# A language-model tower on one core: attention projections of ScalarE in two units, VectorE's steps behind them one unit on, and the output addition ahead of the cell

## The chip, the core and the metric

The kernel runs on one core of a Trainium2 chip. A core has five engines, each with its own instruction queue that it works off strictly in the order in which the program wrote it: TensorE (PE: matrix products), VectorE (DVE: element-wise work and reductions), ScalarE (ACT: activation functions), GpSimd (POOL) and SyncE (SP, here only the issuer of DMA transfers). Queues meet only through semaphores: an instruction that waits for one holds back everything behind it on its engine. The metric is the device time of one execution in microseconds (us).

## The reference

One layer of a small language model over 16 sequences of 512 tokens and a width of 128. Three parts follow each other for each sequence: an embedding with a short Fourier transform, a local attention with 64 summary tokens and 8 heads, and an LSTM as a mixture of 8 experts of which each token takes 2. The LSTM's scan runs over the sequences, so its state passes from sequence to sequence.

```
h = tok(x, ...)                                   # (16, 512, 128)
h = h + attn(_layernorm(h), W_qkv, b_qkv, W_out, b_out)
h = h + ffn(_layernorm(h), router_w, ..., Wi, Wh, b, Wo, bo)

attn:  Q, K, V = split(x @ W_qkv + b_qkv); Q = Q * SCALING
       aw  = softmax(Qw . Kcat);  out_wtok = aw . Vcat            # 64 summary tokens
       w_wtok = softmax(Qf . out_wtok);  w_fea = softmax(Qf . Kseg)  # a window of 17 keys
       out_fea = w_wtok * out_wtok + w_fea . Vseg
ffn:   top_vals, top_idx = top_k(logits, 2);  rw = softmax(top_vals)
       step: gates = xt @ Wi + h @ Wh + b;  i_, f_, g_, o_ = split(gates)
             c = sigmoid(f_) * c + sigmoid(i_) * tanh(g_);  h = sigmoid(o_) * tanh(c)
             y = h @ Wo + bo
```

## The kernel before

**Steps and units.** The main part runs over the 16 sequences (`STEPS`). A step is cut into 32 units (`NG * E`): 8 experts of 4 gates each, expert `e = t // 4` and gate `g = t % 4`. In every unit TensorE computes one gate of one expert for both of a token's choices (1024 columns; `unit_gate`, lines 594, 597 and 599), and ScalarE takes its tanh (`gate_tanh`, line 762). TensorE may be at most two gates ahead of ScalarE, since there are two PSUM halves for gates. VectorE closes an expert over the four units that follow: in a unit with `g == 1` the masked input and the swap of hidden states of the next expert (lines 1108, 1116) and `input_part` (1141), with `g == 2` `chosen` (1162) and `cell` (1149, 1153), with `g == 3` the swap of the cell state (1123), in the next `g == 0` `hidden` (1131). `hidden` needs ScalarE's tanh of the cell (`cell_tanh`, line 769), issued in the unit with `g == 3`.

**Front.** Beside the LSTM of one sequence, the embedding and the attention of the next ones are woven in, in small pieces (`front`). A table per engine (`PE_AT`, `ACT_AT`, `DVE_AT`, `SP_AT`) says in which unit a piece is written into that engine's queue. A negative number belongs to the step before: -5 is unit 27, -4 is unit 28, -3 is unit 29 there. `run_front` puts the pieces in. What sets the order is this table and the order of the calls inside `step` of each engine; there is no scheduler behind it. On VectorE the front piece of a unit stands behind `masked_input`, the swaps and `chosen`, and ahead of `input_part` and `cell`. On ScalarE it stands behind the unit's `gate_tanh` and `cell_tanh`, on TensorE behind the unit's gate.

**The pieces around the change.** TensorE computes query, key and value in unit 27 (line 524). ScalarE moves them out of PSUM: query `qT` (698) and two scaled halves of it, `qz` (703), then key `kw`, `kf` (707, 708) and value `vw`, `vf` (710, 711), all in one go in unit 27; `split` (716, 718) makes the f16 upper parts of key and value a unit later. VectorE waits for `qT` and `kf` for the products `pw` (921, 922), then makes the lower parts of the query (`q_lo`, 926) in unit 28, of key and value (`kv_lo`, 931, 934) in unit 29, and so on through `v_win` (942), `w_max` (946, 948), `s_max` (971), `s_sub`, `w_sum`, `w_out` (961 to 967), up to `p_T`. ScalarE's exponential for the summary tokens (721) waits for `w_max`. `add_y` (1168) adds the LSTM's output of the sequence before to its residual; it waits for four transposes of TensorE (`y_back`, line 618).

**The first step.** Step 0 has a single state per token (512 columns) and no forget gate. Ahead of it the front of sequence 0 and part of that of sequence 1 run alone. In every step a mask for each expert comes by DMA into `masks` before `masked_input` can use it.

Of the kernel before, what the change touches and what calls it, by code (L numbers as in the profile page):

```python
# [5 lines left out]
def lm_tower_kernel(nc, x_ids, frame_ids, emb_table, proj_w, proj_b, w_qkv, b_qkv, w_out, b_out,  # L6
# [46 lines left out]
    Q_SCALE = 2.0 ** 4  # L53


    SP_AT = dict(ids=-16, qbd=-3, vz=1, rows=25, wrow=28)
    PE_AT = dict(emb=-10, xT=-6, qkv=-5, summary=-2, window=0, feature=6, values=12, proj=15, projT=16, x2T=19,
                 logits=21, maskT=25)
    ACT_AT = dict(h=-10, xT=-6, qkv=-5, split=-4, summary=0, window=3, pr_hi=7, feature=8, proj=15, x2T=19,
                  choice=21, maskT=25)  # L60
    DVE_AT = dict(onehot=-14, moments=-9, xn=-8, pw=-4, q_lo=-4, kv_lo=-3, v_win=-2, w_max=-1, s_max=1, s_sub=2, w_sum=3,
                  w_out=4, s_sum=5, s_norm=6, f_max=7, p_lo=8, p_T=9, f_sum=10, f_part=10, attn=13,
                  moments2=16, xn2=17, x_lo=20, choice1=21, choice2=21, weights=22)
    EARLY = 16
    MASKS_AT = 26
    YT_AT, YBACK_AT, YADD_AT = 5, 6, 7
    WT0 = 64
    XM_AT = 30
    ENC0 = 32
# [2 lines left out]
    with ctx:  # L72
# [26 lines left out]
        rows = sb("rows", [P, SEQ])  # L99
# [7 lines left out]
        xn = sb("xn", [P, TILES, D])  # L107
# [7 lines left out]
        ids = prod[0:VOCAB, :].bitcast(i32)  # L115
# [10 lines left out]
        attn = sb("attn", [P, SEQ])  # L126
# [537 lines left out]
        def _(act):  # L664
# [18 lines left out]
            def front(t, b):  # L683
                b1 = b + 1
                if t == ACT_AT["h"]:
                    act.wait_ge(S["emb"], b1)
                    if not is_zero(b):
                        act.wait_ge(S["h2"], b)
                    A(h_sb[:, :, :].rearrange("p t d -> p (t d)"), FA[:, 0, :], ACT.Copy).then_inc(S["hsb"], 1)
                if t == ACT_AT["xT"]:  # L690
                    act.wait_ge(S["xnTp"], b1)
                    A(xnT[:, :], FA[:, 0, :], ACT.Copy).then_inc(S["xnT"], 1)
                if t == ACT_AT["qkv"]:
                    act.wait_ge(s_prep, 3)
                    act.wait_ge(S["qp"], b1)
                    if not is_zero(b):
                        act.wait_ge(S["S"], b)
                    A(qT[:, :], FA[:, 0, :], ACT.Identity, bias=bqkv_sb[:, 0:1], scale=DH ** -0.5).then_inc(S["q"], 1)
                    act.wait_ge(S["q"], b1)
                    if not is_zero(b):  # L700
                        act.wait_ge(S["mwp"], b)
                    for c in range(2):
                        last = A(qz[:, :, c, :, HI], qT[:, NW:SEQ].rearrange("p (j q) -> p j q", q=QB), ACT.Copy,
                                 scale=parq[:, c:c + 1])
                    last.then_inc(S["qhi"], 1)
                    act.wait_ge(S["kp"], b1)
                    A(kw[:, :], FA[:, 1, 0:NW], ACT.Identity, bias=bqkv_sb[:, 1:2])
                    A(kf[:, PAD:PAD + TF], FA[:, 1, NW:SEQ], ACT.Identity, bias=bqkv_sb[:, 1:2]).then_inc(S["k"], 1)
                    act.wait_ge(S["vp"], b1)
                    A(vw[:, :], FB[:, 0:NW], ACT.Identity, bias=bqkv_sb[:, 2:3])  # L710
                    A(vf[:, PAD:PAD + TF], FB[:, NW:SEQ], ACT.Identity, bias=bqkv_sb[:, 2:3]).then_inc(S["v"], 1)
                if t == ACT_AT["split"]:
                    if not is_zero(b):
                        act.wait_ge(S["mout"], 16 * b)
                    act.wait_ge(S["k"], b1)
                    A(khl[:, HI, :], kf[:, :], ACT.Copy, scale=Q_SCALE).then_inc(S["khi"], 1)
                    act.wait_ge(S["v"], b1)
                    A(vp16[:, :, HI], vf[:, :], ACT.Copy, scale=Q_SCALE).then_inc(S["vhi"], 1)
                if t == ACT_AT["summary"]:
                    act.wait_ge(S["dw"], b1)  # L720
                    A(ew[:, :], prod[:, :], ACT.Exp).then_inc(S["ew"], 1)
                if t == ACT_AT["window"]:
                    act.wait_ge(S["dS"], b1)
                    A(pr[:, :], pr[:, :], ACT.Exp, scale=1.0 / (Q_SCALE * Q_SCALE)).then_inc(S["eS"], 1)
                if t == ACT_AT["pr_hi"]:
                    act.wait_ge(S["pn"], b1)
                    A(pr16[:, :, HI], vwin[:, :], ACT.Copy, scale=V_SCALE).then_inc(S["phi"], 1)
                if t == ACT_AT["feature"]:
                    act.wait_ge(S["df"], b1)
                    A(ew[:, 0:TF], prod[:, 0:TF], ACT.Exp).then_inc(S["ef"], 1)  # L730
                if t == ACT_AT["proj"]:
                    act.wait_ge(S["projT"], b1)
                    A(xnT[:, :], FA[:, 1, :], ACT.Identity, bias=bout_sb[:, 0:1]).then_inc(S["projS"], 1)
                if t == ACT_AT["x2T"]:
                    act.wait_ge(S["x2p"], b1)
                    A(x32[:, :], FB[:, :], ACT.Copy).then_inc(S["x32"], 1)
                    A(xs[:, par_of(b), HI, :], FB[:, :], ACT.Copy, scale=V_SCALE).then_inc(S["xhi"], 1)
                if t == ACT_AT["choice"]:
                    act.wait_ge(S["dd"], b1)
                    A(m4[:, 6, :], m4[:, 5, :], ACT.Exp).then_inc(S["ed"], 1)  # L740
                if t == ACT_AT["maskT"]:
                    act.wait_ge(S["mwp"], b1)
                    if not is_zero(b):
                        act.wait_ge(S["mout"], 16 * b)
                    A(mrow[:, :], FB[0:K * E, :], ACT.Copy).then_inc(S["mrow"], 1)
                    if not is_zero(b):
                        act.wait_ge(S["wout"], 16 * b)
                        act.wait_ge(S["ybo"], b)
                    A(wT, FB[WT0:WT0 + E, :], ACT.Copy).then_inc(S["wT"], 1)
# [90 lines left out]
        def _(dve):  # L840
# [293 lines left out]
            def input_part(s, e, first):  # L1134
                dve.wait_ge(s_tanh, gates_to(s, e, 1))
                at_i, at_g = tmp[:, gate_at(I, e), 0:width(s)], tmp[:, gate_at(G, e), 0:width(s)]
                if first:
                    STT(out=C[:, e, 0:SEQ], in0=at_i, scalar=1.0, in1=at_g,
                        op0=ALU.add, op1=ALU.mult).then_inc(s_c, 1)
                    return  # L1140
                STT(out=at_i, in0=at_i, scalar=1.0, in1=at_g,  # L1141
                    op0=ALU.add, op1=ALU.mult).then_inc(s_u, 1)
# [21 lines left out]
            def add_y(s, par):  # L1164
                dve.wait_ge(s_yback, s + 1)
                dve.wait_ge(S["h2"], s + 1)
                flat = h2[:, par, :, :].rearrange("p t d -> p (t d)")
                TT(flat, flat, yp[:, :], ALU.add).then_inc(s_yadd, 1)

            def step(s, par, first, last):  # L1170
                for t in range(NG * E):
                    e, g = t // NG, t % NG

                    if g == 0 and e:
                        hidden(s, e - 1)
                    elif g == 0 and not first:
                        hidden(s - 1, E - 1)
                    if g == 1 and e < E - 1:
                        masked_input(s, e + 1, par, first and e == 0)
                    if g == 1 and e < E - 1 and not first:  # L1180
                        swap_h(s, e + 1)
                    if t == XM_AT and not last:
                        masked_input(s + 1, 0, 1 - par, False)
                        swap_h(s + 1, 0)
                    if t == YADD_AT and not first:
                        add_y(s - 1, 1 - par)
                    if g == 3 and e < E - 1 and not first:
                        swap_c(s, e + 1)
                    elif g == 3 and e == E - 1 and not last:
                        swap_c(s + 1, 0)  # L1190
                    if g == 2 and e:
                        chosen(s, e - 1)
                    elif g == 2 and not first:
                        chosen(s - 1, E - 1)
                    run_front(lambda u, b: front(u, b, b % 2), t, s)
                    if g == 1:
                        input_part(s, e, first)
                    if g == 2 and not first:
                        cell(s, e)
            dve.wait_ge(s_pad, 1)  # L1200
# [110 lines left out]
```

## Time and profile before

| | us |
|---|---|
| median of 3 runs | 1634.19 (1632.33 to 1635.96) |
| the profiled execution's own time | 1635.68 |
| its span, first to last instruction | 1633.9 |
| TensorE busy with products, share of the span | 1550.4, 95% |
| VectorE busy | 1490.9, 91% |
| ScalarE busy | 859.0, 53% |

Busy time is what the profiler's records cover. Matrix products overlap in the records, so TensorE's share overstates how close it is to its limit, and starts should be compared with starts. An instruction of VectorE or ScalarE starts about 0.1 us before the record of the one in front of it ends where nothing is waited for. "Idle" of a row is the time in which the engine did nothing just before that instruction, with the instruction that ended it. The profile's granted clock of TensorE is 0.98 of full speed on the mean, and full from the seventh of 40 slices on. A step of the main part takes 101.0 us, with the same pattern each time.

### The profile page before, as it was taken

What the parts mean: (1) busy time and instruction counts of PE and PEld (TensorE: products, weight loads), DVE (VectorE), ACT (ScalarE), POOL (GpSimd) and SP (SyncE); (2) the same over time, 40 slices, a digit from 0 to 9 for tenths busy, and PEclk for the clock granted to TensorE, in tenths of its full rate; (3) what the DMA queues carried; (4) which work ended last, traced back from release to release, by engine and by line L of the source; (5) the groups of instructions that cost most, each with busy time, mean ns of one, the idle gap of its engine ahead of it and who ended that gap; (6) DMA issues with size and microseconds to landing.
All of it is one profiled execution on the core that took longest, in us unless ns stands there. A gap on an engine that the chain in (4) does not pass through costs nothing.

```text
span 1633.9 us, 21374 instructions
## 1 busy us (share of the span) xinstructions
PE 1550.4 (95%) x7325; PEld 741.7 (45%) x7325; DVE 1490.9 (91%) x2442; ACT 859.0 (53%) x1022; POOL 53.2 (3%) x42
## 2 busy tenths in 40 slices
PE   7767999999999999999999999999999999999998
PEld 3423444444444444444444444444444454444443
DVE  4667999999999999999999999999999999999986
ACT  4445455465555555555455454554555555465454
POOL 1000000000000000000000000000000000000000
PEclk9878999999999999999999999999999999999999
DMA  4144435444464453644435444354543545445453
GB/s 142 17 88 115 129 130 157 132 128 141 127 158 131 138 136 128 152 139 136 142 119 145 150 129 146 115 161 137 138 132 128 151 139 139 138 126 147 130 143 97
DMA packets 252461, 215.54 MB, mean 132 GB/s; under 512 B 131173, under 2 KB 174104, under 8 KB 252353
## 3 DMA queue, kind: packets, MB, share of 16 engines
q1 hardware_dynamic: 252272, 214.16, 45.6%
q8 instruction: 58, 0.95, 0.2%
q14 instruction: 51, 0.41, 0.1%
q10 hardware_dynamic: 80, 0.02, 0.0%
HBM read 73.06 MB, written 4.74 MB: 48 GB/s over the span
## 4 chain that ended last, share of the span: by engine, by line
DVE 61%; issue 16%; PE 13%; ACT 6%; POOL 2%; DMA 1%; SPq 1%; DVEq 0%; ACTq 0%
DVE H L1116 8%; DVE tmp L1149 8%; DVE C L1123 6%; DVE C L1153 5%; DVE tmp L1141 5%; DVE xm L1108 4%; PE gates L597 3%; PE gates L594 3%; DVE H L1131 3%; DVE z L1162 2%; PE gates L599 2%; POOL rstd L1243 2%; DVE xn L915 1%; DVE stats L883 1%; PE yp L605 1%
## 5 line engine op out<-in xcount | busy, mean ns | idle before, releaser
L762 ACT ACTIVATE tmp<-gates,bias_sb 128x1024 f32<-128x1024 f32 (+1 forms) x504 | 533.8, 1063 | 426.0 <-PE gates L599 375.3
L597 PE MATMUL gates<-H,wh_sb 128*128 128x512 f32 x960 | 492.4, 594 | 0.0
L599 PE MATMUL gates<-H,wh_sb 128*128 128x512 f32 x896 | 459.4, 594 | 0.0
L594 PE MATMUL gates<-xm,wi_sb 128*128 128x512 f16 x1512 | 412.3, 382 | 23.7 <-ACT tmp L762 17.6
L594 PEld LDWEIGHTS gates<-xm,wi_sb 128*128 128x128 f16 x1512 | 141.4, 99 | 316.3 <-issue 192.2
L599 PEld LDWEIGHTS gates<-H,wh_sb 128*128 128x128 f32 x896 | 171.1, 191 | 215.7 <-issue 215.7
L769 ACT ACTIVATE tmp<-C 128x1024 f32<-128x1024 f32 (+1 forms) x128 | 128.6, 1004 | 252.3 <-DVE C L1153 245.8
L597 PEld LDWEIGHTS gates<-H,wh_sb 128*128 128x128 f32 x960 | 182.9, 191 | 69.5 <-issue 0.4
L1141 DVE SCALAR_TENSOR_TENSOR tmp<-tmp 128x1024 f32<-128x1024 f32 (+1 forms) x120 | 140.9, 1174 | 18.3 <-ACT tmp L762 18.3
L1123 DVE COPY_PREDICATED C<-masks,Cx 128x1024 f32<-128x1024 uint16 (+1 forms) x120 | 154.4, 1286 | 0.0
L1116 DVE COPY_PREDICATED H<-masks,Hx 128x1024 f32<-128x1024 uint16 (+1 forms) x120 | 152.2, 1268 | 0.0
L1131 DVE SCALAR_TENSOR_TENSOR H<-tmp 128x1024 f32<-128x1024 f32 (+1 forms) x128 | 147.8, 1154 | 3.8 <-ACT tmp L769 3.1
L1153 DVE SCALAR_TENSOR_TENSOR C<-tmp 128x1024 f32<-128x1024 f32 (+1 forms) x120 | 142.7, 1189 | 4.1
L1149 DVE SCALAR_TENSOR_TENSOR tmp<-tmp,C 128x1024 f32<-128x1024 f32 (+1 forms) x120 | 141.4, 1178 | 2.8 <-ACT tmp L762 2.3
L605 PE MATMUL yp<-z,wo_sb 128*128 128x512 f32 x256 | 135.2, 610 | 4.4 <-DVE z L1162 4.4
L1243 POOL TENSOR_TENSOR rstd<-veps,mhalf 128x4 f32<-128x4 f32 x32 | 49.7, 1552 | 1461.7 <-DVE veps L1039 1150.7
L1108 DVE TENSOR_TENSOR xm<-xs,masks 128x1024 f16<-128x1024 f16 x128 | 87.8, 686 | 1.9 <-DMA masks<-mask_scratch 1.9
L1162 DVE TENSOR_TENSOR z<-H,roww 128x512 f32<-128x512 f32 x128 | 87.7, 685 | 1.3 <-PE yp L605 1.2
L605 PEld LDWEIGHTS yp<-z,wo_sb 128*128 128x128 f32 x256 | 47.7, 193 | 70.7 <-issue 59.8
L551 PEld LDWEIGHTS FA<-vwin,diag 128*128 128x128 f16 x1344 | 36.3, 98 | 12.2 <-issue 9.2
L539 PEld LDWEIGHTS FA<-xn,diag 128*128 128x128 f16 x1344 | 38.1, 97 | 8.0 <-issue 5.3
L539 PE MATMUL FA<-xn,diag 128*128 128x32 f16 x1344 | 39.0, 177 | 0.0
(170 smaller groups left out, 1224.5 us busy)
## 6 DMA issues: line engine op xcount, KB each, us to landing
Hx<-H SPq DMA_DIRECT2D x232, 256.0 KB, 2.8
Cx<-C SPq DMA_DIRECT2D x232, 256.0 KB, 2.4
masks<-mask_scratch SPq DMA_DIRECT2D x128, 256.0 KB, 5.1
roww<-mw_scratch SPq DMA_DIRECT2D x128, 256.0 KB, 3.3
diag<-pr SPq DMA_DIRECT2D x64, 112.0 KB, 3.5
diag<-vwin SPq DMA_DIRECT2D x64, 112.0 KB, 3.2
out_dram<-h SPq DMA_DIRECT2D x16, 256.0 KB, 2.6
C<-in_wi SPq DMA_DIRECT2D x1, 2048.0 KB, 10.9
```

The source lines that it names most:

```text
L594: last = mm(fed, wi_sb[:, e, wpart, rows_of], xm[:, e % 2, vpart, :], start=(wpart == HI and vpart == HI), stop=(first and wpart == LO))
L597: last = mm(fed, wh_sb[:, e, rows_of], H[:, e, 0:SEQ], start=False, stop=True)
L599: last = mm(other, wh_sb[:, e, rows_of], H[:, e, SEQ:2 * SEQ], start=True, stop=True)
L605: mm(yp[:, :], wo_sb[:, e, :], z32[:, :], start=False, stop=(e == E - 1)).then_inc(s_y, 1)
L762: A(tmp[:, gate_at(gate, e), 0:width(s)], gates[:, (n - 1) % 2, 0:width(s)], ACT.Tanh, bias=bias_sb[:, e, gate:gate + 1], scale=UNSCALE).t ...
L1108: TT(xm[:, e % 2, :, :], xs[:, par, :, :], mv_, ALU.mult).then_inc(s_xm, 1)
L1116: V.copy_predicated(halves(H[:, e, 0:w]), masks[:, e % 2, 1:2, :].to_broadcast([P, w // SEQ, SEQ]).bitcast(u16), halves(Hx[:, 0:w])).then_ ...
L1123: V.copy_predicated(halves(C[:, e, 0:w]), masks[:, e % 2, 1:2, :].to_broadcast([P, w // SEQ, SEQ]).bitcast(u16), halves(Cx[:, 0:w])).then_ ...
L1131: STT(out=H[:, e, 0:w], in0=tmp[:, gate_at(O, e), 0:w], scalar=1.0, in1=tmp[:, TANH_C, 0:w], op0=ALU.add, op1=ALU.mult).then_inc(s_h, 1)
L1141: STT(out=at_i, in0=at_i, scalar=1.0, in1=at_g, op0=ALU.add, op1=ALU.mult).then_inc(s_u, 1)
L1149: STT(out=at_f, in0=at_f, scalar=1.0, in1=C[:, e, 0:w], op0=ALU.add, op1=ALU.mult).then_inc(s_v, 1)
L1153: STT(out=C[:, e, 0:w], in0=at_f, scalar=0.5, in1=tmp[:, gate_at(I, e), 0:w], op0=ALU.mult, op1=ALU.add).then_inc(s_c, 1)
```

## The change

The table and two calls are changed; the instructions and their sizes stay as they are. ScalarE's `qkv` piece becomes two, `q` in unit 27 and `kv` in unit 28, and its pieces from `split` to `feature` go one unit on. VectorE's pieces from `pw` to `p_T` go one unit on, as do TensorE's `summary`, `window` and `feature`; `f_sum`, `values` and all that follows keep their unit. `add_y` goes from the head of unit 7 into unit 6, between `input_part`'s place and `cell`. SyncE's `qbd` goes one unit on, which passes no other transfer in its queue.

```diff
-    SP_AT = dict(ids=-16, qbd=-3, vz=1, rows=25, wrow=28)
-    PE_AT = dict(emb=-10, xT=-6, qkv=-5, summary=-2, window=0, feature=6, values=12, proj=15, projT=16, x2T=19,
+    SP_AT = dict(ids=-16, qbd=-2, vz=1, rows=25, wrow=28)
+    PE_AT = dict(emb=-10, xT=-6, qkv=-5, summary=-1, window=1, feature=7, values=12, proj=15, projT=16, x2T=19,
...
-    ACT_AT = dict(h=-10, xT=-6, qkv=-5, split=-4, summary=0, window=3, pr_hi=7, feature=8, proj=15, x2T=19,
+    ACT_AT = dict(h=-10, xT=-6, q=-5, kv=-4, split=-3, summary=0, window=4, pr_hi=8, feature=9, proj=15, x2T=19,
...
-    DVE_AT = dict(onehot=-14, moments=-9, xn=-8, pw=-4, q_lo=-4, kv_lo=-3, v_win=-2, w_max=-1, s_max=1, s_sub=2, w_sum=3,
-                  w_out=4, s_sum=5, s_norm=6, f_max=7, p_lo=8, p_T=9, f_sum=10, f_part=10, attn=13,
+    DVE_AT = dict(onehot=-14, moments=-9, xn=-8, pw=-3, q_lo=-3, kv_lo=-2, v_win=-1, w_max=0, s_max=2, s_sub=3, w_sum=4,
+                  w_out=5, s_sum=6, s_norm=7, f_max=8, p_lo=9, p_T=10, f_sum=10, f_part=10, attn=13,
...
-    YT_AT, YBACK_AT, YADD_AT = 5, 6, 7
+    YT_AT, YBACK_AT, YADD_AT = 5, 6, 6
...
                     last.then_inc(S["qhi"], 1)
+                if t == ACT_AT["kv"]:
                     act.wait_ge(S["kp"], b1)
...
-                    if t == YADD_AT and not first:
-                        add_y(s - 1, 1 - par)
                     if g == 3 and e < E - 1 and not first:
                         swap_c(s, e + 1)
...
                     if g == 1:
                         input_part(s, e, first)
+                    if t == YADD_AT and not first:
+                        add_y(s - 1, 1 - par)
                     if g == 2 and not first:
                         cell(s, e)
```

ScalarE's queue at units 27 to 29 of a full step, before. `L698` to `L711` are query, key and value, the first `L762` is unit 28's gate tanh, `L716` and `L718` the split.

```order
L698 ACTIVATE qT<-FA,bqkv_sb 128x512
L703 ACTIVATE pr<-qT,parq 128x28x16 x2
L707 ACTIVATE kw<-FA,bqkv_sb 128x64
L708 ACTIVATE kf<-FA,bqkv_sb 128x448
L710 ACTIVATE vw<-FB,bqkv_sb 128x64
L711 ACTIVATE vf<-FB,bqkv_sb 128x448
L762 ACTIVATE tmp<-gates,bias_sb 128x1024
L716 ACTIVATE xn<-kf 128x464
L718 ACTIVATE ew<-vf 128x464
```

The same place now; lines past 705 have moved on by one, so `L763` is the gate tanh and `L709` writes `kf`.

```order
L698 ACTIVATE qT<-FA,bqkv_sb 128x512
L703 ACTIVATE pr<-qT,parq 128x28x16 x2
L763 ACTIVATE tmp<-gates,bias_sb 128x1024
L708 ACTIVATE kw<-FA,bqkv_sb 128x64
L709 ACTIVATE kf<-FA,bqkv_sb 128x448
L711 ACTIVATE vw<-FB,bqkv_sb 128x64
L712 ACTIVATE vf<-FB,bqkv_sb 128x448
L763 ACTIVATE tmp<-gates,bias_sb 128x1024
L717 ACTIVATE xn<-kf 128x464
L719 ACTIVATE ew<-vf 128x464
```

One gate tanh now stands between the query's halves and the key, and one between the value and the split.

VectorE's queue from `hidden` of expert 6 (unit 28) to the cell of expert 7 (unit 30), before. `L921` waits for `kf`.

```order
L1131 SCALAR_TENSOR_TENSOR H<-tmp 128x1024
L921 TENSOR_TENSOR prod<-qT,kw 128x64
L922 TENSOR_TENSOR prod<-qT,kf 128x64x7
L926 SCALAR_TENSOR_TENSOR pr<-qT,parq,pr 128x28x16 x2
L931 SCALAR_TENSOR_TENSOR xn<-kf,xn 128x464
L934 SCALAR_TENSOR_TENSOR ew<-vf,ew 128x464
L1141 SCALAR_TENSOR_TENSOR tmp<-tmp 128x1024
L1108 TENSOR_TENSOR xm<-xs,masks 128x1024
L1116 COPY_PREDICATED H<-masks,Hx 128x1024
L1162 TENSOR_TENSOR z32<-H,roww 128x512
L942 STREAM_TRANSPOSE vwin<-ew 128x896
L1149 SCALAR_TENSOR_TENSOR tmp<-tmp,C 128x1024
```

The same place now.

```order
L1132 SCALAR_TENSOR_TENSOR H<-tmp 128x1024
L922 TENSOR_TENSOR prod<-qT,kw 128x64
L923 TENSOR_TENSOR prod<-qT,kf 128x64x7
L927 SCALAR_TENSOR_TENSOR pr<-qT,parq,pr 128x28x16 x2
L1142 SCALAR_TENSOR_TENSOR tmp<-tmp 128x1024
L1109 TENSOR_TENSOR xm<-xs,masks 128x1024
L1117 COPY_PREDICATED H<-masks,Hx 128x1024
L1163 TENSOR_TENSOR z32<-H,roww 128x512
L932 SCALAR_TENSOR_TENSOR xn<-kf,xn 128x464
L935 SCALAR_TENSOR_TENSOR ew<-vf,ew 128x464
L1150 SCALAR_TENSOR_TENSOR tmp<-tmp,C 128x1024
```

The two products still stand directly behind `hidden`: unit 28 holds nothing else of VectorE's. The lower parts of key and value now come after the input part, the masked input, the swap and `chosen`, and the window transpose of `v` after the cell.

VectorE's queue from unit 1 to unit 2 and around unit 6 also changes; in unit 6, before, with `L1168` the output addition:

```order
L992 TENSOR_TENSOR vwin<-pr,wred 128x896
L1149 SCALAR_TENSOR_TENSOR tmp<-tmp,C 128x1024
L1153 SCALAR_TENSOR_TENSOR C<-tmp 128x1024
L1168 TENSOR_TENSOR h2<-h2,yp 128x512
L1123 COPY_PREDICATED C<-masks,Cx 128x1024
```

And now:

```order
L989 RECIPROCAL wred<-wred 128x28
L1169 TENSOR_TENSOR h2<-h2,yp 128x512
L1150 SCALAR_TENSOR_TENSOR tmp<-tmp,C 128x1024
L1154 SCALAR_TENSOR_TENSOR C<-tmp 128x1024
L1124 COPY_PREDICATED C<-masks,Cx 128x1024
```

The addition stands ahead of the two instructions of the cell, and `s_norm` (`L992`) has gone behind them.

## Rows read from the trace of the kernel before

**Rows 1.** Busy time of the engines in one full step.
```profile
core 0: us, PE busy (x) PEld busy (x) DVE busy (x) ACT busy (x) POOL busy (x), PEclk, DMA share, GB/s
870.00:971.00 101.00, 98.57 (x461) 47.23 (x460) 96.70 (x154) 54.56 (x62) 3.31 (x2) 1.00 0.47 138
```

**Rows 2.** All waits of VectorE in that step: total, times, longest.
```profile
DVE prod L921 <- ACT kf L708: 1.5, 1, 1.5
DVE xn L915 <- POOL rstd L1243: 0.9, 1, 0.9
DVE tmp L1141 <- ACT tmp L762: 0.3, 1, 0.3
DVE xn L931 <- ACT xn L716: 0.2, 1, 0.2
```

**Rows 3.** The two longest waits of TensorE's products in that step.
```profile
PE gates L594 <- ACT tmp L762: 1.3, 3, 0.8
PE yp L612 <- DVE h L1168: 0.5, 1, 0.5
...
```

**Rows 4.** Waits of VectorE for the key: whole span, then the first 150 us.
```profile
DVE prod L921 <- ACT kf L708: 30.5, 16, 6.6
...
DVE prod L921 <- ACT kf L708: 8.1, 2, 6.6
```

**Rows 5.** ScalarE in order of time, units 27 to 29: start, duration.
```profile
956.66 1.06 ACT L769 ACTIVATE tmp<-C 128x1024 f32<-128x1024 f32 x1 [1.73 <-DVE C L1153]
...
959.62 0.28 ACT L707 ACTIVATE kw<-FA,bqkv_sb 128x64 f32<-128x64 f32 x1
...
961.03 1.12 ACT L762 ACTIVATE tmp<-gates,bias_sb 128x1024 f32<-128x1024 f32 x1
962.02 0.60 ACT L716 ACTIVATE xn<-kf 128x464 f16<-128x464 f32 x1
...
963.08 1.12 ACT L762 ACTIVATE tmp<-gates,bias_sb 128x1024 f32<-128x1024 f32 x1
```

**Rows 6.** VectorE in order of time, the same units.
```profile
957.76 1.22 DVE L1131 SCALAR_TENSOR_TENSOR H<-tmp 128x1024 f32<-128x1024 f32 x1
960.52 0.28 DVE L921 TENSOR_TENSOR prod<-qT,kw 128x64 f32<-128x64 f32 x1 [1.53 <-ACT kf L708]
...
961.20 1.30 DVE L926 SCALAR_TENSOR_TENSOR pr<-qT,parq,pr 128x448 f16<-128x448 f32 x2
962.66 0.64 DVE L931 SCALAR_TENSOR_TENSOR xn<-kf,xn 128x464 f16<-128x464 f32 x1 [0.16 <-ACT xn L716]
...
964.23 1.23 DVE L1141 SCALAR_TENSOR_TENSOR tmp<-tmp 128x1024 f32<-128x1024 f32 x1 [0.27 <-ACT tmp L762]
```

**Rows 7.** TensorE in order of time, the gates of units 29 and 30.
```profile
960.92 1.02 PE L599 MATMUL gates<-H,wh_sb 128*128 128x512 f32 x2
962.21 0.82 PE L594 MATMUL gates<-xm,wi_sb 128*128 128x512 f16 x3 [0.26 <-ACT tmp L762]
```

**Rows 8.** VectorE and ScalarE around the exponential for the summary tokens.
```profile
872.11 0.69 DVE L948 TENSOR_TENSOR prod<-FB,red 128x512 f32<-128x512 f32 x1
872.72 1.22 DVE L1131 SCALAR_TENSOR_TENSOR H<-tmp 128x1024 f32<-128x1024 f32 x1
872.84 0.63 ACT L721 ACTIVATE ew<-prod 128x512 f32<-128x512 f32 x1 [0.53 <-DVE prod L948]
873.86 0.68 DVE L1108 TENSOR_TENSOR xm<-xs,masks 128x1024 f16<-128x1024 f16 x1
...
875.65 1.09 DVE L971 TENSOR_REDUCE wred<-FA 128x28 f32<-128x896 f32 x1
```

**Rows 9.** VectorE in step 0, units 4, 5 and 13.
```profile
103.84 0.68 DVE L961 TENSOR_REDUCE red<-prod 128x64 f32<-128x512 f32 x1
...
107.38 0.69 DVE L1108 TENSOR_TENSOR xm<-xs,masks 128x1024 f16<-128x1024 f16 x1 [1.95 <-DMA masks<-mask_scratch]
...
121.67 1.66 DVE L1020 SCALAR_TENSOR_TENSOR attn<-FA,par_sb,attn 128x224 f32<-128x224 f32 x4 [0.95 <-PE FA L551]
```

More of the change, by code:

```diff
@@ L692, in front @@
                     A(xnT[:, :], FA[:, 0, :], ACT.Copy).then_inc(S["xnT"], 1)
-                if t == ACT_AT["qkv"]:
+                if t == ACT_AT["q"]:
                     act.wait_ge(s_prep, 3)
```

## The prediction, written before the changed kernel ran

> **What bounds the kernel now.** I read first the busy times of one full step, then who waited for whom in that step on VectorE and on TensorE, then both engines and ScalarE in order of time around unit 28. A step takes 101.0 us, and in it TensorE is busy 98.6, VectorE 96.7, ScalarE 54.6 us [rows 1]. TensorE looks fuller, so the waits must decide.
>
> VectorE has four waits in a step, 1.53 + 0.90 + 0.27 + 0.16 = 2.9 us [rows 2, 6]. The 1.3 to 1.4 us left to 101.0 are gaps between instructions that depend on each other. None of the four is ended by TensorE. The longest, before the products with the key, ends when ScalarE has written `kf`. ScalarE is then in an unbroken run that starts with the tanh of the cell, and that tanh was released by VectorE's own cell (L1153) [rows 5]. The 0.9 us is for GpSimd's `rstd`, which VectorE's `veps` releases. The two small ones wait for ScalarE's queue, which is still working off the block with query, key and value. So the loop that sets a step's length goes VectorE to ScalarE and back, and each microsecond of waiting on VectorE counts. TensorE's own waits (1.3 us for the gate tanh, 0.5 us for the output addition [rows 3]) are ended by engines that are in turn late because of VectorE: it has room.
>
> The reader should see one thing in rows 5 and 6 together. VectorE ends `hidden` and has nothing else to do before the products: it starts them at 960.52, 0.9 us after ScalarE began with the key at 959.62.
>
> **The change part by part.** No instruction is added or dropped, so all that can change is waiting.
>
> 1. *The key comes later.* In ScalarE's queue unit 28's gate tanh now stands between the query's halves and the key. Such a tanh holds the queue for 962.02 - 961.03 = 0.99 us [rows 5]. Its gate has been ready for long: unit 29's last product starts at 960.92 [rows 7], one gate, some 3.2 us with the expert's output, behind it. So the tanh starts where the key started, at 959.62, and the key at 960.61. On VectorE the products still stand right behind `hidden`, since unit 28 has nothing else. They start at 960.52 + 0.99 = 961.51, and the wait of 1.53 us becomes 2.52. `q_lo` could run at once but stands behind the products. Cost: +0.99.
>
> 2. *Two small waits go.* The input part of expert 7 now follows `q_lo` directly. `q_lo` takes 962.66 - 0.16 - 961.20 = 1.30 us to the next start, so the input part can start at 961.20 + 0.99 + 1.30 = 963.49. It needs unit 29's tanh, which no longer stands behind the split. That one starts when key and value are out, 961.03 - 959.62 = 1.41 us after the key's start, so at 960.61 + 1.41 = 962.02, and with 964.23 - 963.08 = 1.15 from its start to its consumer it is there at 963.17. No wait: -0.27. The lower parts of key and value come some 3 us later, when the split is long done: -0.16. Check: input part at 963.49 plus the 1.30 us of these two (962.66 to 964.23 - 0.27) still owed is 964.79, against 964.23 before: +0.56 a step.
>
> 3. *Everything up to `p_T` a unit later.* It is the same work in another order, and before the cell of unit 10 the two orders have met again. A debt is harmless as long as nobody waits. `S` is ready for `s_max`; the masks and the copies of state that SyncE issues behind `vz` leave about 2.5 us later and still have some 4 us. `p_T` ends about when TensorE wants `values`; a stall of 0.3 us there falls before one of 0.8 us that TensorE has for the tanh of that cell anyway. The tight place is the exponential, a rival below. I take 0.
>
> 4. *Output addition ahead of the cell.* It costs the same on VectorE. The transposes that it needs ended some 3 us before VectorE gets there. It takes away TensorE's 0.5 us [rows 3], behind which nothing of VectorE waits. I take 0; the cell's end moves by +0.6 for the addition and -1.0 for `s_norm`, which went behind it.
>
> 5. *Step 0.* VectorE waits 1.95 us for a mask in unit 5 [rows 9], whose DMA is issued behind `vz` and so behind TensorE's window product, which waits for a DMA as before. Today `w_out` runs ahead of this wait, 107.38 - 1.95 - 103.84 = 1.6 us; now it comes behind. Some 0.95 us come back at the wait before the attention [rows 9]: +0.6. The key's delay at its end: +0.5, the tanh there being half as wide, and VectorE then being held by TensorE for a while. From nothing to 2 us for both.
>
> Ahead of step 0 ScalarE has no gate tanh between the parts, so two of the 16 waits for the key (8.1 us) stay as they are; 22.4 of 30.5 us are 14 waits, 2.4 in step 0 and 13 of 1.54 [rows 4]. Sum: 13 x 0.56 = 7.3, + 0.6 + 0.5 = 8.4 us. In the last two steps TensorE takes over as the bound, but it enters them as late as VectorE's cell let it. The profiled execution took 1635.68 us, which gives 1644.1; the median of the runs is 1.5 us lower, so 1642.6 us.
>
> Bounds of a step's term: if neither small wait went, 0.99; if the tanh cost only what a half as wide one costs and both went, 0.3. With step 0 the sum is 4 to 15 us: 1638 to 1649.
>
> **A rule of the skill.** ScalarE is busy 54% of the step and makes VectorE wait 1.53 us [rows 1, 2]. The Trainium skill, "Perfetto Trace Analysis", section "Optimizing Scalar/DVE Operations", says that where Scalar isn't saturated but causes bubbles on other engines, breaking up its work may let it end sooner. The block is broken up here, but the piece that VectorE waits for is the one behind the break; by the rule the time would be that of the third rival.
>
> **The rivals.**
>
> *Slower by more, through the exponential (15%).* `w_max` now stands behind `hidden`, directly ahead of masked input and swap of unit 1. ScalarE's exponential waits for it, with the tanh of unit 1 behind, and VectorE's input part needs this tanh. From the start of `w_max`'s second instruction ScalarE needs 0.73 to the exponential (872.84 - 872.11), 0.53 for it and 1.15 for the tanh: 2.4 us. VectorE has 0.61 + (875.65 - 873.86 = 1.79) = 2.4 us of work in between [rows 8]. The margin is nil; today this tanh waits for its gate instead. If 0.4 us is missing a step, 14 x 0.4 = 5.6 us more: 1648. It decides from a wait of 0.2 us on.
>
> *No change (12%).* The key's delay is taken up elsewhere: TensorE, not held at the gate of unit 30 (0.26 us [rows 7]), would set the pace, and VectorE's lateness would end in slack. Then 1634. Against it: no wait of VectorE in a step is for TensorE [rows 2].
>
> *The waits shrink (3%).* If the break let VectorE find the key ready, 1.53 + 0.27 + 0.16 = 1.96 us a step would go: 14 x 1.96 = 27 us, 1607 us. This needs other work of VectorE's in unit 28, and the queue has none.
>
> *TensorE is the bound (7%).* Then its waits count: the 0.5 us before `yp` goes, of the 1.3 us for gate tanh the 0.26 in unit 30 and about 0.3 in unit 10, where `pr_hi` no longer stands ahead of the tanh. 1.1 x 14 = 15 us, so 1619 us. For it speaks only the higher busy time [rows 1]. The Trainium skill, "Perfetto Trace Analysis", section "Identifying the Most-Contended Engine", takes the highest occupancy for the bound, but warns that TensorE's share isn't a good measure; the waits of the trace agree with the warning.
>
> **How the numbers follow.** 63% for the forecast at 1642.6 (its own range 1638 to 1649). My range is 1636 to 1650: it leaves out the two faster cases, most of the unchanged one, and the upper end of the exponential. A measurement of this kernel tells about 0.2%, 3.3 us, from no change. Slower by more than that: the forecast but for its lowest end (61%), the exponential (15%) and a little: 78%. Within: 14%. Faster: 8%.
>
> **What would show it.** Right: VectorE's wait before the products with the key near 2.5 us in each full step, the ones before the input part of expert 7 and before the lower part of the key gone, a step of 101.5 to 101.6 us, no wait for the output addition on TensorE, and the same busy times. Wrong: a key wait that has not grown, or that has while a step still takes 101.0 us. A wait of the input part for a gate tanh in unit 1 would show the exponential.

## The result, and the profile after

The changed kernel takes 1651.84 us (median of 4 runs, 1648.42 to 1654.15) against 1635.08 us (1632.33 to 1636.5) for the kernel before beside it: a ratio of 1.0103, interval [1.0079, 1.0126]. It is slower, as forecast, but by 16.8 us where the sum said 8.4, and it lies above the range (1636 to 1650).

The profiled execution took 1652.79 us with a span of 1651.0 us, 17.1 us more than before in either figure. The page has these busy times.

```profile
PE 1564.9 (95%) x7325; PEld 746.8 (45%) x7325; DVE 1487.3 (90%) x2442; ACT 863.2 (52%) x1022; POOL 53.2 (3%) x42
```

TensorE has 14.5 us more busy time than before and VectorE 3.6 us less, at the same work. So some of TensorE's instructions have become longer. One full step (it runs from one pair of products with the key to the next, 102.37 us), and 3.85 us inside it, in windows with their busy times, answer to [rows 1]:

```profile
core 0: us, PE busy (x) PEld busy (x) DVE busy (x) ACT busy (x) POOL busy (x), PEclk, DMA share, GB/s
970.93:1073.30 102.37, 99.96 (x461) 47.76 (x460) 96.43 (x154) 54.84 (x64) 3.31 (x2) 0.98 0.48 136
1022.95:1026.80 3.85, 3.85 (x8) 1.46 (x9) 3.81 (x8) 0.95 (x1) 0.00 (x0) 0.62 0.87 187
```

VectorE's and TensorE's waits of a step (total, times, longest), against [rows 2, 3]:

```profile
DVE prod L922 <- ACT kf L709: 2.5, 1, 2.5
DVE h L1030 <- PE FB L560: 1.1, 1, 1.1
DVE xn L916 <- POOL rstd L1244: 0.9, 1, 0.9
...
PE gates L594 <- ACT tmp L763: 2.1, 1, 2.1
```

Three readings. The wait for the key has grown as forecast, and the two small ones are gone. There is a wait that was hardly there before: the residual addition `h` (L1030) now waits 1.1 us for TensorE's transposes. And TensorE, which waited three times at gates and once for the output addition, waits once, for 2.1 us. Over the whole span the same two of VectorE's read, against [rows 4]:

```profile
DVE prod L922 <- ACT kf L709: 44.6, 16, 6.6
DVE h L1030 <- PE FB L560: 16.3, 14, 2.7
```

Before, that second group was 4.0 us in 4 waits.

VectorE and ScalarE at the place of the change, start and duration, against [rows 5, 6]:

```profile
969.02 1.10 ACT L763 ACTIVATE tmp<-gates,bias_sb 128x1024 f32<-128x1024 f32 x1
970.01 0.31 ACT L708 ACTIVATE kw<-FA,bqkv_sb 128x64 f32<-128x64 f32 x1
...
971.44 1.14 ACT L763 ACTIVATE tmp<-gates,bias_sb 128x1024 f32<-128x1024 f32 x1
...
970.95 0.28 DVE L922 TENSOR_TENSOR prod<-qT,kw 128x64 f32<-128x64 f32 x1 [2.55 <-ACT kf L709]
...
971.62 1.32 DVE L927 SCALAR_TENSOR_TENSOR pr<-qT,parq,pr 128x448 f16<-128x448 f32 x2
972.82 1.23 DVE L1142 SCALAR_TENSOR_TENSOR tmp<-tmp 128x1024 f32<-128x1024 f32 x1
...
976.34 0.65 DVE L932 SCALAR_TENSOR_TENSOR xn<-kf,xn 128x464 f16<-128x464 f32 x1
976.90 0.68 DVE L935 SCALAR_TENSOR_TENSOR ew<-vf,ew 128x464 f16<-128x464 f32 x1
977.46 1.22 DVE L1150 SCALAR_TENSOR_TENSOR tmp<-tmp,C 128x1024 f32<-128x1024 f32 x1
```

The tanh holds ScalarE for 970.01 - 969.02 = 0.99 us ahead of the key, and the wait is 2.55 us where 2.52 was forecast.

Now TensorE around the gate of unit 14 in the same step: the last product of unit 13, the wait, and what comes behind it.

```profile
1019.85 1.02 PE L599 MATMUL gates<-H,wh_sb 128*128 128x512 f32 x2
1022.95 0.82 PE L594 MATMUL gates<-xm,wi_sb 128*128 128x512 f16 x3 [2.08 <-ACT tmp L763]
1023.61 1.65 PE L597 MATMUL gates<-H,wh_sb 128*128 128x512 f32 x2
1025.05 1.91 PE L599 MATMUL gates<-H,wh_sb 128*128 128x512 f32 x2
1026.76 1.07 PE L594 MATMUL gates<-xm,wi_sb 128*128 128x512 f16 x3
...
1033.46 0.60 PE L560 MATMUL FB<-ident,xnT 128*128 128x128 f32 x4
```

And the same gate in the kernel before:

```profile
1013.29 0.82 PE L594 MATMUL gates<-xm,wi_sb 128*128 128x512 f16 x3 [0.77 <-ACT tmp L762]
1013.95 1.02 PE L597 MATMUL gates<-H,wh_sb 128*128 128x512 f32 x2
1014.81 1.02 PE L599 MATMUL gates<-H,wh_sb 128*128 128x512 f32 x2
```

After a wait of 2.08 us pairs that take 1.02 us take 1.65 and 1.91 us, and in the window from 1022.95 the granted clock is 0.62 on the mean: for most of it TensorE runs at the lower of its two levels, 1.2 GHz instead of 2.4. The four runs agree: the fastest (1648.42 us) has the highest mean clock, 0.978, and the slowest (1654.15 us) the lowest, 0.971. From the gate's start to the next gate's it takes 1026.76 - 1022.95 = 3.81 us instead of 1015.67 - 1013.29 = 2.38, which makes it 1.4 us late. Some ten microseconds later VectorE comes for the transposes of L560 and waits:

```profile
1034.10 0.69 DVE L1030 TENSOR_TENSOR h<-FB,h_sb 128x512 f32<-128x512 f32 x1 [1.12 <-PE FB L560]
```

The kernel holds its own counter-example. The step from 255.75 on, in the same execution:

```profile
307.59 0.82 PE L594 MATMUL gates<-xm,wi_sb 128*128 128x512 f16 x3 [2.08 <-ACT tmp L763]
308.25 1.02 PE L597 MATMUL gates<-H,wh_sb 128*128 128x512 f32 x2
309.11 1.02 PE L599 MATMUL gates<-H,wh_sb 128*128 128x512 f32 x2
...
317.68 0.69 DVE L1030 TENSOR_TENSOR h<-FB,h_sb 128x512 f32<-128x512 f32 x1
```

The same wait of 2.08 us, the full clock behind it, no wait of VectorE, and that step takes 101.27 us where those with the low clock take 102.0 to 102.6. In 12 of the 14 steps with this wait (2.08 us, 1.96 in the first) the clock falls behind it, and in the same 12, and no other, L1030 waits 0.89 to 1.13 us. These 12 are the last 12, one after the other.

The budget, from the starts of VectorE's long product with the key (`kf`): the third is at 154.60 instead of 153.24 us (+1.4, step 0 and ahead), the last at 1482.88 instead of 1466.07. The 13 steps between grew by 15.45 us. 11 of them have the new wait, 11.4 us in sum; the other 4.1 us are 0.31 a step. Behind the last product it is +0.3, although the twelfth such wait stands there. Together 17.1 us.

### The profile page after: what moved, and what is told of

The parts are those of the page before. It is cut to its first block, busy times and chain, and to the rows that moved or that the text cites. A ratio compares the mean times of both kernels' runs of the same rounds, so it can differ in the third digit from the quotient of the medians.

```text
span 1651.0 us, 21374 instructions
## 1 busy us (share of the span) xinstructions
PE 1564.9 (95%) x7325; PEld 746.8 (45%) x7325; DVE 1487.3 (90%) x2442; ACT 863.2 (52%) x1022; POOL 53.2 (3%) x42
## 4 chain that ended last, share of the span: by engine, by line
DVE 60%; PE 18%; issue 13%; ACT 5%; POOL 2%; DMA 1%; SPq 1%; DVEq 0%; ACTq 0%
DVE tmp L1150 7%; DVE H L1117 6%; DVE tmp L1142 6%; DVE C L1124 5%; PE gates L597 5%; PE gates L594 4%; DVE H L1132 4%; DVE C L1154 4%; PE gates L599 3%; DVE xm L1109 3%; DVE z L1163 3%; ACT tmp L763 2%; POOL rstd L1244 2%; PE yp L605 2%; DVE xn L916 1%
## 5 line engine op out<-in xcount | busy, mean ns | idle before, releaser
L763 ACT ACTIVATE tmp<-gates,bias_sb 128x1024 f32<-128x1024 f32 (+1 forms) x504 | 533.6, 1062 | 375.3 <-PE gates L599 328.7
L597 PE MATMUL gates<-H,wh_sb 128*128 128x512 f32 x960 | 498.5, 601 | 0.0
L599 PE MATMUL gates<-H,wh_sb 128*128 128x512 f32 x896 | 468.1, 605 | 0.0
L599 PEld LDWEIGHTS gates<-H,wh_sb 128*128 128x128 f32 x896 | 173.8, 194 | 219.7 <-issue 219.7
L1142 DVE SCALAR_TENSOR_TENSOR tmp<-tmp 128x1024 f32<-128x1024 f32 (+1 forms) x120 | 142.1, 1184 | 13.6 <-ACT tmp L763 13.6
L922 DVE TENSOR_TENSOR prod<-qT,kw 128x64 f32<-128x64 f32 x16 | 4.4, 275 | 44.6 <-ACT kf L709 44.6
```

Source lines behind the costliest of these rows:

```text
L597: last = mm(fed, wh_sb[:, e, rows_of], H[:, e, 0:SEQ], start=False, stop=True)
L599: last = mm(other, wh_sb[:, e, rows_of], H[:, e, SEQ:2 * SEQ], start=True, stop=True)
L763: A(tmp[:, gate_at(gate, e), 0:width(s)], gates[:, (n - 1) % 2, 0:width(s)], ACT.Tanh, bias=bias_sb[:, e, gate:gate + 1], scale=UNSCALE).t ...
L1142: STT(out=at_i, in0=at_i, scalar=1.0, in1=at_g, op0=ALU.add, op1=ALU.mult).then_inc(s_u, 1)
```

## The experiments

Theory A: what the forecast missed is the clock that falls behind the joined wait of TensorE. Rival B: it comes from the new order itself (TensorE's transposes are late because their inputs or its queue are). Ratios are to the kernel before, on the same chip.

**Filling the wait (e_fill).** The changed kernel, with work for TensorE in the gap and nothing else touched: 8 dummy products, whose result is overwritten before anyone reads it.

```diff
+                if t == 13 and not is_zero(b):
+                    pe.wait_ge(S["df"], b1)
+                    for _ in range(8):
+                        mm(FB[:, :], identb[:, :], identb[:, :].rearrange("p (a k) -> p a k", a=1)
+                           .to_broadcast([P, TILES, P]), start=True, stop=True)
```

> The changed kernel with 8 dummy products (512 columns, bf16, into a PSUM tile that is free there) in TensorE's queue behind the gate of unit 13, where it now waits 2.08 us for unit 12's gate tanh; they fill about 1.7 us of that wait. Theory A, the clock: in 11 of 13 full steps TensorE runs at the half clock right behind this wait, and its lateness makes VectorE wait 1.1 us before the attention's residual addition (line 1030). With the wait filled the clock stays full, a step takes 101.3 instead of 102.4 us, and the time is 1652 - 11 x 1.07 = 1640 us. Theory B, the order: the new wait before line 1030 comes from the pieces moved a unit on, whatever the clock: 1652 us as the changed kernel, or up to 2 us more.

Measured: 1639.68 us, ratio 1.0032 [1.0021, 1.0042]. A kernel with more work is 12 us faster than the changed one (each beside the kernel before, ratios 1.0032 and 1.0103). A window that holds the gate of unit 14, and TensorE's rows there (lines past 553 are 5 on, so L599 is the gate's first line):

```profile
1019.11:1021.50 2.39, 2.39 (x8) 1.08 (x9) 2.39 (x5) 0.95 (x1) 0.00 (x0) 1.00 0.72 252
```

```profile
1016.87 1.89 PE L557 MATMUL FB<-identb 128*128 128x512 bf16 x8
1019.11 0.82 PE L599 MATMUL gates<-xm,wi_sb 128*128 128x512 f16 x3 [0.35 <-ACT tmp L768]
1019.77 1.02 PE L602 MATMUL gates<-H,wh_sb 128*128 128x512 f32 x2
```

The clock stays full, no step has a wait for the transposes, and the full steps take 101.27 us on the mean of the last 12 (101.02 before). The expected 1640 for A came, the 1652 for B did not.

**A smaller filling (e_fill3).** The same with `range(3)`.

> As e_fill but with 3 dummy products instead of 8: 0.65 us of TensorE's 2.08 us wait ahead of the gate of unit 14 is filled, about 1.4 us stays open, behind it the gate. Theory A, the clock, as a matter of how long TensorE stands still in one piece: 1.4 us is near the 0.8 us of the kernel before, where the clock stayed full, so 1640 us as with 8. If a wait of 1.4 us already lets the clock fall: up to 1652 us. Theory B, that the 8 dummies helped in another way than by the clock (they hold gates back): somewhere between, with a full clock and a wait before the residual addition.

Measured: 1638.96 us, 1.0032 [1.002, 1.0044]. TensorE's wait in a step:

```profile
PE gates L599 <- ACT tmp L768: 1.4, 1, 1.4
```

With 1.4 us still open the clock stays full behind the wait in all 14 steps, and the gain is that of 8 dummies, as theory A expected.

**The control (e_before_fill).** The same 3 dummies in the kernel before.

> Control for the filler: the kernel before with the same 3 dummy products into FB behind the gate of unit 13. Theory A (the filler mends only the fallen clock of the changed kernel, and the kernel before has none): within 0.1% of the kernel before, 1635 us, the steps at 101.0. Rival B (the dummies speed the kernel up by some other way, as by keeping PSUM or the queue busy): 1625 to 1630. If the dummies load TensorE where it has no room: 1640 or more.

Measured: 1636.54 us, 1.0001 [0.998, 1.0022]. By themselves they bring nothing. Most steps take 101.1 us. In two steps the clock fell here behind unit 10, and there L1034 (the same addition) waited 0.83 and 0.85 us: in the kernel before such a fall costs only 0.2 us there. The dummies take up most of the 0.8 us at unit 14 in which TensorE otherwise makes up for it.

**The output addition back (e_yadd_back).** The changed kernel with this part undone.

```diff
-    YT_AT, YBACK_AT, YADD_AT = 5, 6, 6
+    YT_AT, YBACK_AT, YADD_AT = 5, 6, 7
...
+                    if t == YADD_AT and not first:
+                        add_y(s - 1, 1 - par)
                     if g == 3 and e < E - 1 and not first:
                         swap_c(s, e + 1)
...
-                    if t == YADD_AT and not first:
-                        add_y(s - 1, 1 - par)
```

> The changed kernel with the output addition back at the head of unit 7, behind the cell. It tells what the addition's move did by itself. Theory A, the clock: TensorE waits again about 0.3 us for the addition in unit 9, so its one long wait at unit 14 gets shorter (1.6 to 2.1 us); if that is enough for the clock to stay full, 1640 us, otherwise 1652. Theory B, the order: nothing of VectorE waits for it, so 1652 us within 2.

Measured: 1648.24 us, 1.0095 [1.0077, 1.0113]. The waits of a step at its low clock:

```profile
PE gates L594 <- ACT tmp L763: 2.1, 1, 2.1
...
DVE h L1030 <- PE FB L560: 1.1, 1, 1.1
...
PE yp L612 <- DVE h L1169: 0.2, 1, 0.2
```

The joined wait doesn't need the addition's move; the move of the other pieces makes it, and TensorE's wait for the addition goes down to 0.2 us all the same. The time lies between the 1640 and the 1652 of the two theories. The clock falls in 10 of 14 steps; where it does not, they take 101.2 to 101.3 us.

**The output addition alone (e_before_yadd).** The kernel before, with only this part done.

> The kernel before with one part of the change alone: the output addition stands in unit 6 between the input part and the cell. Theory A (my reading of the changed kernel: the addition costs VectorE nothing, TensorE loses its 0.5 us before the transposes of the output, and its other waits are spread enough for the clock to stay up): 1633 to 1636 us, the steps at 101.0 us, no wait of VectorE for FB of 1 us. Rival B (taking TensorE's wait of 0.5 us away lets it run on into one longer wait at a gate, and the clock falls behind it, as in the changed kernel): about 1645 us with a wait of 2 us at a gate and of 1.1 us of VectorE before the residual addition.

Measured: 1636.57 us, 1.0012 [1.0003, 1.0021]. Both theories have a piece of it. The wait of 0.5 us goes, and TensorE waits 1.4 to 1.5 us in one piece at unit 10 in each of 13 steps. In 4 of these the clock falls, as here, and VectorE then waits 0.5 to 0.7 us at L1029:

```profile
391.99 1.17 PE L594 MATMUL gates<-xm,wi_sb 128*128 128x512 f16 x3 [1.46 <-ACT tmp L762]
392.95 1.92 PE L597 MATMUL gates<-H,wh_sb 128*128 128x512 f32 x2
...
415.56 0.69 DVE L1029 TENSOR_TENSOR h<-FB,h_sb 128x512 f32<-128x512 f32 x1 [0.71 <-PE FB L560]
```

These four sum to 2.6 us; most other steps take 101.1 us, against 101.0 before. So the addition ahead of the cell is not a gain, and costs at most what the clock takes.

**Key and value back in unit 27 (e_kv_back).** The changed kernel with `kv=-5`; everything else stays moved.

> The changed kernel with ScalarE's key and value part back in unit 27, ahead of unit 28's gate tanh; all else as changed. VectorE's wait for the key goes from 2.52 back to 1.5 us, but its input part of expert 7 then waits about 0.7 us for unit 29's tanh: 0.3 us a step, 13 x 0.3 = 4 us. Theory A, the clock: VectorE is then earlier against TensorE at unit 14, the wait there shrinks towards 1.7 us and the clock stays full: 1652 - 4 - 12 = 1636 us. Theory B, the order: only the 4 us: 1648 us.

Measured: 1640.33 us, 1.0038 [1.0026, 1.005]. VectorE's wait for the key and TensorE's waits in a step:

```profile
PE gates L594 <- ACT tmp L763: 2.2, 2, 1.9
...
DVE prod L922 <- ACT kf L709: 1.5, 1, 1.5
```

The key wait is back at 1.5 us, yet most steps still take 101.2 us: the input part now waits 0.4 to 0.8 us for its tanh, behind the unbroken block. The wait at gate 14 is there (1.9 to 2.1 us), but the clock falls in 3 of 14 steps only, and each of those has the 0.9 to 1.1 us at L1030 and takes 101.9 to 102.4 us. So neither theory had it whole: the step is not the 0.3 us shorter that both took, and the wait is not much shorter, but the clock falls in 3 steps instead of 12. With 2.0 us less in the first full step that makes most of the 12 us against the changed kernel.

**ScalarE's split of the block alone (e_key).** The kernel before with the block in two units and only what has to follow it.

```diff
-    ACT_AT = dict(h=-10, xT=-6, qkv=-5, split=-4, summary=0, window=3, pr_hi=7, feature=8, proj=15, x2T=19,
+    ACT_AT = dict(h=-10, xT=-6, q=-5, kv=-4, split=-3, summary=0, window=3, pr_hi=7, feature=8, proj=15, x2T=19,
...
-    DVE_AT = dict(onehot=-14, moments=-9, xn=-8, pw=-4, q_lo=-4, kv_lo=-3, v_win=-2, w_max=-1, s_max=1, s_sub=2, w_sum=3,
+    DVE_AT = dict(onehot=-14, moments=-9, xn=-8, pw=-3, q_lo=-3, kv_lo=-2, v_win=-2, w_max=-1, s_max=1, s_sub=2, w_sum=3,
```

> The kernel before with only the first part of the change: ScalarE's query part in unit 27, key and value part in unit 28, split in unit 29; on VectorE the products with the key and q_lo in unit 29 and kv_lo in unit 30; all later pieces, TensorE's and the output addition as before. It prices the key's delay alone. Theory A: VectorE's wait for the key grows from 1.53 to 2.55 us, the waits of 0.16 and 0.27 go, and the new order drops some 0.3 us of gaps between dependent instructions: +0.3 us a step, 13 x 0.3, with 0.5 in step 0: 1639 us, at a full clock. Prediction as put down before (+0.56 a step): 1642 us. If this part alone brings the half clock at unit 14 too: 1651 us.

Measured: 1640.54 us, 1.0041 [1.0026, 1.0056]. Waits of a step:

```profile
DVE prod L922 <- ACT kf L709: 2.6, 1, 2.6
...
PE gates L594 <- ACT tmp L763: 1.5, 3, 0.8
...
PE yp L612 <- DVE h L1169: 0.8, 1, 0.8
```

The steps take 101.57 us on the mean of the last 12, +0.55 against before; the term of the forecast was 0.56, and theory A's +0.3 did not come. It comes in the changed kernel at the full clock, in part for the order around the lower parts: there the cell starts 977.46 - 976.90 = 0.56 us after the second of them, in e_key the window transpose, which reads what it writes, starts 1067.49 - 1066.73 = 0.76 us after it. TensorE's waits stay apart. The clock fell at unit 10 in three steps, and cost VectorE 0.15 us in one of them.

**Where the key wait can be filled (e_xm29, and three with it).** If VectorE's wait for the key counts, the masked input and the swap of the next step's first expert (units 30 and on) can stand ahead of the products. In the kernel before:

```diff
-    DVE_AT = dict(onehot=-14, moments=-9, xn=-8, pw=-4, q_lo=-4, kv_lo=-3, v_win=-2, w_max=-1, s_max=1, s_sub=2, w_sum=3,
+    DVE_AT = dict(onehot=-14, moments=-9, xn=-8, pw=-3, q_lo=-3, kv_lo=-3, v_win=-2, w_max=-1, s_max=1, s_sub=2, w_sum=3,
...
-    XM_AT = 30
+    XM_AT = 29
```

> The kernel before with one thing changed that aims at the wait for the key: VectorE's masked input and swap of the next step's expert 0 go from unit 30 to unit 29 and the products with the key and q_lo behind them, so that 1.8 us of work stand between hidden and the products. If VectorE's loop sets the step, the wait of 1.5 us goes and the one of 0.16 too: 14 x 1.7 = 24 us less, 1611 us. If TensorE takes over, which waits 2.4 us of a step of 101.0: about 1620 us. If masks or copies of state then come too late: 1635 us.

Measured: 1626.61 us, 0.9957 [0.9945, 0.9969], the fastest kernel of this study. The wait for the key is gone, but only 8 of the 24 or so us arrive, since the input part now waits for gate tanhs, and in four steps the masked input for its mask (2.7 us in sum):

```profile
DVE tmp L1141 <- ACT tmp L762: 1.6, 2, 1.3
...
DVE xn L915 <- POOL rstd L1243: 0.9, 1, 0.9
```

The same edit in the changed kernel with 8 dummies (e_xm29_after_fill):

> The changed kernel with the 8 dummy products of e_fill and with the masked input and swap of the next step's expert 0 in unit 29 ahead of the products with the key. VectorE's wait for the key of 2.55 us is then filled by 1.8 us of work: a step of 101.2 - 1.8 = 99.4 us, 1639.7 - 25 = 1615 us. If TensorE's queue is the bound by then, as in e_xm29 where a step stayed at 100.6 us: about 1626 us.

Measured: 1630.72 us, 0.9976 [0.9964, 0.9988]. And with key and value back in unit 27 as well (e_xm29_kv_fill):

> As e_xm29_after_fill, with ScalarE's key and value part back in unit 27. The key is there 1 us earlier, so the products don't wait, but the input part of expert 7 waits 0.5 us for unit 29's tanh: a step of 99.2 us and 1613 us by VectorE's loop, 1626 us if TensorE is the bound.

Measured: 1635.45 us, 1.0007 [0.9998, 1.0016]. In both the cell of the next step's expert 0 (unit 2) now waits for its tanh, 1.2 us in the first and 1.8 us in this one:

```profile
DVE tmp L1155 <- ACT tmp L768: 1.8, 1, 1.8
```

The lower bounds (1611 to 1615 us), which took VectorE's loop alone, were missed each time. TensorE, dummies included, is busy 100.1 and 99.8 of 101.0 us in these two, and feeds these tanhs; that it is then the bound fits, but no run without its dummies was made in these two.

The best one with the addition ahead of the cell (e_xm29_yadd):

> A try for a better kernel: the kernel before with the masked input and the swap of the next step's expert 0 in unit 29 ahead of the products with the key (as in the earlier run, 1626.6 us), and the output addition ahead of the cell. There TensorE's waits decided part of the step; the addition's place takes away TensorE's wait of 0.4 us before the transposes of the output. If TensorE is the bound there: 1626.6 - 14 x 0.3 = 1622 us. If VectorE is: 1626 us. If the merged wait lets the clock fall: 1636 us.

Measured: 1631.77 us, 0.9976 [0.9967, 0.9986], slower than without. By the ratios (0.9976 and 0.9957) that is 3 us. TensorE's waits join to 1.0 us at unit 10, and the clock falls in one of 14 steps, which costs 0.6 us; the rest stays open.

Over the kernels, TensorE's longest wait in a full step and how often the lower clock came right behind it:

| kernel | wait, us | clock falls behind it | VectorE waits for the transposes there |
|---|---|---|---|
| changed | 2.0 to 2.1 | 12 of 14 steps | 12, of 0.9 to 1.1 us |
| e_yadd_back | 2.0 to 2.1 | 10 of 14 | 10, of 0.9 to 1.1 |
| e_kv_back | 1.9 to 2.1 | 3 of 14 | 3, of 0.9 to 1.1 |
| e_before_yadd | 1.4 to 1.5 | 4 of 13 | 4, of 0.5 to 0.7 |
| e_fill3, behind dummies | 1.3 to 1.4 | 0 of 14 | none |
| e_xm29_yadd | 1.0 | 1 of 14 | 1, of 0.6 |

At other places after the first full step the clock fell at unit 10, behind two short waits: in two steps of the kernel before, where VectorE waited 0.2 us, in two of e_before_fill and in three of e_key.

The falls are not independent draws. In the changed kernel the granted clock is 1.00 in the 0.2 us ahead of 409.47 us and 0.50 behind it, and the same at 1535.87 us: between them lie eleven steps, and the low stretches begin 102.40 us apart each time, 0.2 to 1.2 us behind the end of the wait. A step with a fall takes 102.0 to 102.6 us, so the wait comes back to nearly the same place; in e_yadd_back nine falls follow each other in this way. A step at the full clock takes 101.3 us, and the next wait comes 1.1 us earlier against that beat. So when the wait comes seems to count, and not only how long it is: in this kernel the two steps without a fall had the same wait at another place. This is read off the rows; no run moved the wait alone.

## Why the prediction was half right

**Step 1, the key: right.** 2.52 us forecast, 2.55 measured.

**Step 2, the small waits: right, and a little too dear.** They went. But I gave `q_lo` and the two lower parts 1.30 us each to the next start, as in [rows 6], where each stands ahead of a wait. Without one, the next instruction starts before their record ends: 972.82 - 971.62 = 1.20 us, and 977.46 - 976.34 = 1.12 us. That is 0.28 us less (0.10 for `q_lo`, 0.18 for the other two), and a step at the full clock takes +0.25 to +0.3 us (e_fill, e_fill3) instead of +0.56. In the sum it is 3 to 4 us too much (13 x 0.3 = 3.9 by these steps). The +0.55 of e_key agrees with the 0.56 partly because 0.2 us of this saving is lost in its order.

**Steps 3 and 4, TensorE: this is where the forecast failed.** Step 3 said that a stall of TensorE "falls before one of 0.8 us that TensorE has for the tanh of that cell anyway", and step 4 took 0 for taking away the 0.5 us "behind which nothing of VectorE waits". Both are right of the first order: a TensorE that is early gains nothing and costs nothing. What I missed is that its waits do not vanish, since VectorE's loop still sets the pace; they go to the next rendezvous. In the kernel before 0.26 us at unit 30, 0.49 ahead of the output, 0.30 at unit 10 and 0.77 at unit 14 were 1.82 us in four pieces; now it is one piece of 2.08. The 0.26 us more is the growth of the step at the full clock, 101.27 against 101.02: TensorE's work has stayed the same, 98.5 us in the step from 255.75 on and 98.6 before, so its idle time grows by what the step grows. e_yadd_back and e_before_yadd divide the blame: step 3's pieces one unit on give the 2.08 us without the addition's move, and the addition's move alone gives a wait of 1.45 us and 2 us of time. Behind the joined wait the clock falls, TensorE is 1.4 us late, and only then does VectorE wait for it. Up to the last product eleven such waits are 11.4 us, for which the prediction had no term: it does not speak of TensorE's clock at all. e_fill shows that the clock is the cause, and not the order alone: the same order with the gap filled is 12 us faster.

**Step 5, step 0: of the right size in this pair, but not shown.** +1.1 forecast, +1.4 measured up to its end, the mask wait being 4.2 us instead of 1.95 [rows 9]. But up to the third product with the key e_before_yadd has the instructions of the kernel before and starts it at 150.32 us, not 153.24, and e_yadd_back has those of the changed kernel and starts it at 151.52 us, not 154.60. Two profiles of the same order lie 3 us apart there, so a term of 1 us can't be told.

**The sum** with these sizes: 1.4 us ahead, 4.1 in the 13 steps, 11.4 for the waits behind the low clock, 0.3 at the end: 17.2 by rounded figures, 17.1 measured. The forecast missed by 8.4 us and not by 11 or 12 because step 2 was 3.2 us too dear (7.3 against 4.1); that was luck.

**The rivals.** The exponential did not appear: over the whole span the waits before the input part are 13.6 us in 9, fewer than the 18.3 us in 22 before. TensorE as the bound was ruled out by the same waits; but "no wait of VectorE in a step is for TensorE", true of the kernel before, was read as if it would stay true. The waits did not shrink. The Trainium skill, "Perfetto Trace Analysis", section "Optimizing Scalar/DVE Operations", speaks of breaking up instructions, which may allow work to be completed sooner; here a run of unbroken instructions was parted and the awaited piece stood behind the break, and the trace has 2.55 us for 1.53.

What stays open: why nearly the same wait was followed by the full clock in 2 steps of the changed kernel and in 11 of e_kv_back. Where it falls against the beat of 102.40 us and its length (1.93 to 2.00 us in ten of those 11, 2.01 to 2.08 in the 3 with a fall) may both have a part; no run tells them apart.

## What to carry to other kernels

An engine that isn't the bound still has to wait somewhere: an edit that removes one of its waits moves it to the next meeting point, so add up where its idle time will lie after the edit. Several short waits of TensorE joined into one were followed by the lower clock in many steps, which makes an engine with room the one that is waited for; where they can't be kept apart, a little work in the gap is a cheap remedy. And a wait costs its length plus the overlap that the instruction ahead of it loses, about 0.1 us here.

## What the hardware showed that was not expected

- Eight dummy products (1.89 us of TensorE) in every full step made the changed kernel 12 us faster, three did the same, and three did nothing in the kernel before.
- Behind a single wait of 2.1 us, in a step with 99.96 us of 102.37 busy, the granted clock was at its lower level for most of the next 3.85 us (mean 0.62), in 12 steps of 14.
- Of two kernels with the same gap at the same unit the clock fell in 12 steps of the one and in 3 of the other, with 0.1 us less of wait in most.
- The 12 falls followed each other without a gap, 102.40 us apart, in steps of 102.0 to 102.6 us: a step with a fall is about as long as the distance from one fall to the next.
